# Key tiles 5, 6 and 7 of the product with V in one interleaved group, exponential 0 before the evacuation, small loads in step 0, and experts' products in pairs

## The reference

```python
x = L0_attn_resid_stream                       # (4, 1024, 128), f32
x = x + attn(layernorm(layernorm(x), ln_w, ln_b))
x = x + moe(layernorm(x))
# attn: 16 heads of 64, causal softmax(q k^T / 8) v, then W_o and b_o
# moe, token by token:
spikes_enc = sigmoid(y @ enc_W + enc_b)        # 128 -> 256
cont = spikes_enc @ s2c_W + s2c_b              # -> 64
logits = tanh(cont @ rW1 + rb1) @ rW2 + rb2    # -> 8 experts
w = top-2 of softmax(logits), scaled to sum 1
h = relu(cont @ We1[e] + be1[e]); out = sum_e w_e (h @ We2[e] + be2[e])
spikes_moe = sigmoid(out @ c2s_W + c2s_b)      # 64 -> 256
decoded = sigmoid(spikes_moe @ dec_W + dec_b)  # -> 128
result = layernorm(decoded, ln_g, ln_b)
```

## Time and profile before

| | us |
|---|---|
| median of 3 runs | 1065.34 |
| lowest and highest | 1065.0, 1068.29 |
| the profiled execution | 1063.64 |
| span of its trace | 1061.6 |
| busy PE, DVE, ACT, POOL | 1005.0, 863.3, 725.0, 739.3 |

### The profile page before, as it was taken

How to read it: one execution, slowest core, us unless ns; L and a number is a source line. 1 busy time by engine, 2 the same in 40 slices (tenths; PEclk the granted TensorE clock), 3 DMA queues, 4 the chain that set the end, 5 groups by cost and what they waited for, 6 DMA issues and landing times.

```text
span 1061.6 us, 50267 instructions
## 1 busy us (share of the span) xinstructions
PE 1005.0 (95%) x19084; PEld 760.5 (72%) x19084; DVE 863.3 (81%) x2052; ACT 725.0 (68%) x1540; POOL 739.3 (70%) x725
## 2 busy tenths in 40 slices
PE   4799999999999999999999999999999978999985
PEld 2577777777777777777777777777777766555543
DVE  6888888888888888888888888888888876557573
ACT  3666777777777777777777777777777755768673
POOL 5797777777777777777777777777777733444653
PEclk8999999999999999999999999999999988999997
DMA  7678888988888888888888888888888864132422
GB/s 164 165 202 212 208 211 205 207 207 208 206 205 204 208 205 205 206 203 203 204 204 204 205 202 205 203 205 201 204 201 206 207 137 87 42 91 51 99 51 69
DMA packets 133022, 188.78 MB, mean 178 GB/s; under 512 B 46976, under 2 KB 60288, under 8 KB 132992
## 3 DMA queue, kind: packets, MB, share of 16 engines
q1 hardware_dynamic: 132992, 188.40, 74.6%
HBM read 133.39 MB, written 21.36 MB: 146 GB/s over the span
## 4 chain that ended last, share of the span: by engine, by line
PE 62%; DVE 14%; issue 12%; DMA 4%; ACT 4%; POOL 2%; SPq 1%; ACTq 1%; DVEq 0%; POOLq 0%
PE ZB L758 24%; PE SPS L732 12%; PE SPS L733 9%; DVE PTZ L1056 5%; PE ZB L777 4%; DVE SSB L1094 3%; PE ZB L714 3%; PE ZB L784 3%; DMA VR<-gate_scratch 2%; ACT PRL L1394 2%; PE ZB L708 1%; DMA gate_scratch<-PRS 1%; POOL X L628 1%; PE SPS L916 1%; DVE PTZ L1251 1%
## 5 line engine op out<-in xcount | busy, mean ns | idle before, releaser
L1094 DVE CUSTOM_DVE_ANT_0 SSB<-SPS,MASK 128x640 f32<-128x640 f32 (+7 forms) x512 | 370.8, 746 | 60.0 <-issue 31.2
L1394 ACT ACTIVATE PRL<-SSB,NM 128x640 f32<-128x640 f32 (+3 forms) x256 | 253.3, 989 | 140.1 <-DVE NM L1094 140.1
L732 PE MATMUL SPS<-KHP,QS 128*128 (+3 forms) x768 | 306.8, 407 | 13.0 <-DVE NM L1094 7.8
L758 PE MATMUL ZB<-PTZ,VR 32*64 32x256 f32 (+3 forms) x12288 | 276.7, 306 | 6.5 <-DVE PTZ L1056 6.2
L1056 DVE STREAM_TRANSPOSE PTZ<-PRL 128x640 f32<-128x640 f32 (+3 forms) x256 | 257.6, 1025 | 0.1
L758 PEld LDWEIGHTS ZB<-PTZ,VR 32*64 32x64 f32 x12288 | 222.2, 131 | 49.2 <-issue 37.2
L733 PE MATMUL SPS<-KLP,QS 128*128 (+3 forms) x768 | 256.6, 343 | 0.0
L1394 ACT ACTIVATE PRS<-SSB,NM 128x128 f32<-128x128 f32 (+3 forms) x256 | 143.2, 562 | 90.3 <-DVE NM L1094 90.3
L732 PEld LDWEIGHTS SPS<-KHP,QS 128*128 128x128 f32 x768 | 145.5, 190 | 80.6 <-issue 47.5
L534 POOL TENSOR_TENSOR PTZ<-PTZ,RSB 128x512 f32<-128x512 f32 x64 | 81.2, 1292 | 132.5 <-ACT PTZ L1405 132.2
L515 POOL TENSOR_TENSOR QS<-RAW,QS 64x512 fp32r<-64x512 f32 x128 | 165.5, 1293 | 10.3
(11 more groups left out here) (178 smaller groups left out, 1215.8 us busy)
## 6 DMA issues: line engine op xcount, KB each, us to landing
VR<-v_scratch SPq DMA_DIRECT2D x248, 256.0 KB, 7.3
KHP<-KHP SPq DMA_DIRECT2D x64, 256.0 KB, 3.6
KLP<-KLP SPq DMA_DIRECT2D x64, 256.0 KB, 4.5
v_scratch<-V SPq DMA_DIRECT2D x32, 512.0 KB, 7.7
RSB<-rcp_scratch SPq DMA_DIRECT2D x64, 256.0 KB
XTB<-xt_scratch SPq DMA_DIRECT2D x62, 256.0 KB, 4.6
XW<-xt_scratch SPq DMA_DIRECT2D x30, 512.0 KB, 8.3
VR<-gate_scratch SPq DMA_DIRECT2D x32, 256.0 KB, 4.7
```

What stands on the lines that cost most here:

```text
L732: pe.matmul(SP_[n % 2][:, o + c0:o + c1], q, kh[:, c0:c1], start=True, stop=False)
L758: last = pe.matmul(ZB[h * DH:(h + 1) * DH, i, t0 * TR:QT * TR], VR[rows, j, kt, h * DH:(h + 1) * DH], turned_block(h, kt, j, rows, t0), st ...
L1094: v.tensor_tensor_reduce(out=SSB[n % 2][:, 0:w], in0=SP_[n % 2][:, o:o + w], in1=MASK[:, S - w:S], scale=1.0, scalar=BIG, op0=ALU.add, op1 ...
L1394: act.activation(exps_of(n), SSB[n % 2][:, 0:w], ACT.Exp, bias=NM[:, col:col + 1], scale=-1.0, accum_out=L[:, col:col + 1]).then_inc(exp_d ...
```

## The change

Five edits:
1. Values of key tiles 5, 6 and 7 are one group of `last_values`, in twelve rounds; its semaphore counts three tiles at its end. After step 31: values(4), logits, values(5,6,7).
2. In the steps of the loop ScalarE makes exponential 0 before it evacuates qk(0).
3. In the beginning the first spreads are split by head, scores(0) and (1) wait each for their own, and the statistics of batch 2 come ahead of the key splits.
4. Eleven small loads go to a new buffer SMALL (40 columns, set to zero once by VectorE) and are issued by SP in step 0, before `store_xt(2)`. `load_router` issues 9 loads instead of 15, `load_experts` 7 instead of 12.
5. In the chunks the hidden products come in pairs ahead of the experts' groups, and ScalarE's order follows.

```diff
-        ENCB, S2CB, RB1 = BV[:, 0:2], BV[:, 2:3], BV[:, 3:4]
-        RW2, RB2, BE1 = BV[:, 8:16], BV[:, 16:24], BV[:, 24:32]
-        C2SB, BE2 = BV[:, 32:34], BV[:, 64:64 + E // 2]
+        SMALL = sb("SMALL", [P, 40])
+        ENCB, S2CB, RB1 = SMALL[:, 0:2], SMALL[:, 2:3], SMALL[:, 3:4]
+        RW2, RB2, BE1 = SMALL[:, 8:16], SMALL[:, 16:24], SMALL[:, 24:32]
+        C2SB, BE2 = SMALL[:, 32:34], SMALL[:, 34:34 + E // 2]
...
             def store_xt(b):
                 sp.wait_ge(xt_ready, 2 * b + 2)
                 sp.dma_start(xt_dram[:, b * S:(b + 1) * S], XST[b]).then_inc(xt_stored[b], DMA)
-            spread(sp, 0, 0, 0)
+            for h in range(2):
+
+                sp.wait_ge(k_split, h + 1)
+                for x in (KH[0], KL[0]):
+                    sp.dma_start(x[0:DH, h, 0:CH].bitcast(F32), x[DH:P, h, 0:CH].bitcast(F32)).then_inc((head_spread, keys_spread[0])[h], DMA)
             sp.wait_ge(pool_const, 3)
             stage(sp, 1)
             spread(sp, 0, 0, 1)
...
                 spread_v(sp, it, half, par, 1)
                 store_v(sp, it + 1, 1 - par)
                 if first:
+                    load_small()
                     store_xt(2)
                     store_xt(3)
                     for b in range(1, B):
...
-                loads = [(ENCW, a["enc_W"]), (ENCB, a["enc_b"].rearrange("(m p) -> p m", p=P)),
...
-                         (C2SB, a["c2s_b"].rearrange("(m p) -> p m", p=P)),
-                         (S2CB[0:M], col(a["s2c_b"])), (S2CB[M:P], col(a["s2c_b"])),
...
-                         (RB1[0:M], col(a["rb1"])), (RB1[M:P], col(a["rb1"]))]
...
                     sp.dma_start(dst, src, allow_slow_non_contiguous=True).then_inc(f_loaded, DMA)
...
+            def load_small():
+                sp.wait_ge(small_set, 1)
+                loads = [(ENCB, a["enc_b"].rearrange("(m p) -> p m", p=P)),
+                         (C2SB, a["c2s_b"].rearrange("(m p) -> p m", p=P)),
+                         (S2CB[0:M], col(a["s2c_b"])), (S2CB[M:P], col(a["s2c_b"])),
+                         (RB1[0:M], col(a["rb1"])), (RB1[M:P], col(a["rb1"])),
+                         (RW2[0:M], a["rW2"]), (RB2, a["rb2"].partition_broadcast(P)),
+                         (BE1, a["be1"].rearrange("e h -> h e")),
+                         (BE2[0:M], a["be2"].rearrange("(p h) m -> h m p", h=2)[0]),
+                         (BE2[M:P], a["be2"].rearrange("(p h) m -> h m p", h=2)[1])]
...
+                    sp.dma_start(dst, src, allow_slow_non_contiguous=True).then_inc(f_small, DMA)
...
             def load_experts():
...
-                        [(RW2[0:M], a["rW2"]), (RB2, a["rb2"].partition_broadcast(P)),
-                         (BE1, a["be1"].rearrange("e h -> h e")),
-                         (W2, a["We2"].rearrange("e h m -> h e m")),
+                        [(W2, a["We2"].rearrange("e h m -> h e m")),
...
-                         (BE2[0:M], a["be2"].rearrange("(p h) m -> h m p", h=2)[0]),
-                         (BE2[M:P], a["be2"].rearrange("(p h) m -> h m p", h=2)[1]),
...
                     sp.dma_start(dst, src, allow_slow_non_contiguous=True).then_inc(f_late, DMA)
...
                 if last:
+                    gp.wait_ge(f_small, FFN_SMALL * DMA)
                     gp.wait_ge(f_loaded, FFN_LOADS * DMA)
...
-            if blocks == (QT - 2, QT - 1):
+            if blocks == (QT - 3, QT - 2, QT - 1):
...
-            work = [[(QT - 2, j) for j in range(n)] + [(QT - 1, j) for j in range(i + 1)] for i in range(n)]
-            for r in range(2 * n):
+            work = [[(QT - 3, j) for j in range(n)] + [(QT - 2, j) for j in range(n)] + [(QT - 1, j) for j in range(i + 1)] for i in range(n)]
+            for r in range(3 * n):
                 for i in range(n):
-                    done = [-(-len(work[i]) * k // (2 * n)) for k in (r, r + 1)]
+                    done = [-(-len(work[i]) * k // (3 * n)) for k in (r, r + 1)]
...
-            last.then_inc(pv_done, 2)
+            last.then_inc(pv_done, 3)
...
-                    if n in (0, UNITS // 2):
+                    if first and it == 0 and n < 2:
+                        pe.wait_ge((head_spread, keys_spread[0])[n], SPREADS * DMA)
+                        pe.wait_ge(q_split, n + 1)
+                    elif n in (0, UNITS // 2):
...
             values(3, 4)
...
-            values(5)
-            values(6, 7)
+            values(5, 6, 7)
...
             pe_values(pe, it, 2, 3)
...
-            pe_values(pe, it, 4, 5)
+            pe_values(pe, it, 4)
...
             pe_logits(pe, 0)
-            pe_values(pe, it, 6, 7)
+            pe_values(pe, it, 5, 6, 7)
...
                 pe_hidden(pe, c, par, 1)
                 if not last:
                     pe_encode(pe, c + 1)
-                pe_hidden(pe, c, par, 2)
                 if first:
+                    pe_hidden(pe, c, par, 2)
                     pe_out(pe, STEPS - 1, 0, Z)
                     pe_out(pe, STEPS - 1, 1, MB)
                     pe.wait_ge(out_copied, STEPS * 2 - 1)
-                pe_experts(pe, c, 0)
-                pe_hidden(pe, c, par, 3)
-                if not first:
+                    pe_experts(pe, c, 0)
+                    pe_hidden(pe, c, par, 3)
+                else:
+                    pe_hidden(pe, c, par, 2)
+                    pe_hidden(pe, c, par, 3)
+                    pe_experts(pe, c, 0)
                     pe_c2s(pe, c - 1, 0)
+                if not last:
+                    pe_cont(pe, c + 1)
                 pe_hidden(pe, c, par, 4)
-                if not last:
-                    pe_cont(pe, c + 1)
+                pe_hidden(pe, c, par, 5)
                 if not first:
                     pe_c2s(pe, c - 1, 1)
                 pe_experts(pe, c, 1)
-                pe_hidden(pe, c, par, 5)
                 if not last:
                     pe_router(pe, c + 1, 1 - par)
                 pe_hidden(pe, c, par, 6)
+                pe_hidden(pe, c, par, 7)
                 if not first:
                     pe_decode(pe, c - 1)
                 if not last:
                     pe_logits(pe, c + 1)
                 pe_experts(pe, c, 2)
-                pe_hidden(pe, c, par, 7)
                 if not last:
                     pe_norm_turn(pe, c + 2)
                 pe_experts(pe, c, 3)
...
+            v.memset(SMALL[:, :], 0.0).then_inc(small_set, 1)
             norm_stats(v, 0)
...
             norm_stats(v, 1)
+            norm_stats(v, 2)
             for s in range(2):
...
-            norm_stats(v, 2)
             norm_stats(v, 3)
...
                 exps_to(2, 7)
             else:
                 act_exp(act, it - 1, 1 - par, UNITS - 1)
+                exps_to(0, 1)
                 qk(0)
-                exps_to(0, 1)
                 qk(1)
                 exps_to(1, 2)
                 qk(2)
...
                 hidden(c, 3)
                 if not first:
                     out_hidden(c - 1, 0)
+                if not last:
+                    cont(c + 1, 1 - par)
                 hidden(c, 4)
-                if not last:
-                    cont(c + 1, 1 - par)
+                hidden(c, 5)
                 if not first:
                     out_hidden(c - 1, 1)
-                hidden(c, 5)
                 if not last:
                     routed(c + 1)
                 hidden(c, 6)
+                hidden(c, 7)
                 if not first:
                     decoded(c - 1)
                 if not last:
                     exps(c + 1)
-                hidden(c, 7)
                 if not last:
                     turn_of(c + 2)
                 if first:
```

More of the change, by code:

```diff
@@ L218, in build_program @@
         keys_spread = [sem(f"keys_spread{c}") for c in range(2)]
+        head_spread = sem("head_spread")
         qk_filled = sem("qk_filled"); qk_evac = sem("qk_evac")
@@ L231, in build_program @@
         out_filled = sem("out_filled"); out_copied = sem("out_copied"); out_evac = sem("out_evac")
+        small_set = sem("small_set"); f_small = sem("f_small")
         f_loaded = sem("f_loaded"); f_late = sem("f_late"); f_high = sem("f_high"); f_weights = sem("f_weights"); zeroed = sem("zeroed")
@@ L284, in staged_count @@
             return it * (3 * DMA) + 2 * DMA
-        FFN_LOADS, FFN_LATE = 15, 12
+        FFN_SMALL, FFN_LOADS, FFN_LATE = 11, 9, 7
         def stage_x(sp, it, c):
@@ L434, in load_router @@
                 sp.wait_ge(zeroed, 2)
-                loads = [(ENCW, a["enc_W"]), (ENCB, a["enc_b"].rearrange("(m p) -> p m", p=P)),
+                loads = [(ENCW, a["enc_W"]),
                          (S2CW[:, :, 0:M], a["s2c_W"].rearrange("(m p) c -> p m c", p=P)),
@@ L438, in load_router @@
                          (DECW, a["dec_W"].rearrange("(m p) d -> p m d", p=P)),
-                         (C2SB, a["c2s_b"].rearrange("(m p) -> p m", p=P)),
-                         (S2CB[0:M], col(a["s2c_b"])), (S2CB[M:P], col(a["s2c_b"])),
```

(20 more changed lines are left out.)

## The result

The changed kernel takes 1056.69 us (median of 4 runs, 1054.79 to 1058.98) against 1066.82 for the kernel before beside it: a ratio of 0.9911, 95% interval 0.9884 to 0.9939. That is 9.5 us less, with an interval from 6.5 to 12.4. The forecast was 1056.4. Run once more beside three variants, it gave 1058.16 and 0.9924 (0.9895 to 0.9954).

A forecast was written before the change was run, and what follows sets the result against it. PE, busy 756.9 of the attention loop's 763 us, was taken to bind. Terms -7.8 - 1.5 + 1.9 - 1.5 + 0 + 0 = -8.9 took 1063.64 to 1054.7; 1.7 for the median gave 1056.4 us, range 1048.0 to 1063.0.

The forecast's parts named there:

- the cover by mask(1): VectorE in the loop: with exponential 0 early, mask(2) is held only by mask(1), starting at 508.47, not 509.01.
- the 0.27: PE before values(0) in the loop: 0.27 us per step free to win, 29 x 0.27 = -7.8 us.
- GpSimd's addition as the cover of the late evacuation: Loop: qk(0)'s evacuation comes about 0.6 us later, but GpSimd, its reader, is adding outputs from 508.35 to 510.86.
- no difference: Rival for the whole kernel: the loop's 0.27 does not arrive and the load chain costs; 1064.2 us, chance 0.09.
- no wait behind the later semaphore: Loop: tile 5's semaphore comes some 1.1 us later for VectorE's transpose of unit 10; cost 0, 0.3 us cover.
- a token 0.05 per step: Loop, values of key tiles 5, 6, 7 in one group: 0.05 us saved per step, -1.5 us in all.
- columns that bind: Rival on the group of tiles 5, 6, 7: half or more of 0.60 us won, 1048.6 or below; chance 0.12.
- 15.4 ns a record: Rival on the group of tiles 5, 6, 7: slower than 12.4 ns, +15.5 us, total 1073.4; chance 0.07.
- the small loads in step 0: Eleven loads on SP ahead of X's stores delay values(0) of step 2: +1.9 us, ends 0 and +6.8.
- stores late: Step 0: X's first store moves from 53.34 to 60.1, so the stores land at 65.3 instead of 63.3.
- fewer and earlier transfers should shorten it: Last step, PE's 3.39 us stall in the last values group: shortened by -1.5 us, ends 0 and -3.4.
- PE's 6.1 us of waits lie beside it: Experts' chunks: the gates' loop sets the period, not PE's relu waits; term 0, ends -6.1 and +1.0.

The follow-up runs named there:

- the last experiment: Kernel before with exponential 0 early and experts' pairs, plus the experts' twelve loads issued behind V's four pieces: 1056.87 us, ratio 0.9905.
- the single runs: Kernel before with one edit alone each: exponential 0 early 1057.75 us, values of tiles 5, 6, 7 1067.01, small loads 1068.32, experts' pairs 1062.04.

## Why the prediction was right or wrong

**Right: exponential 0.** Forecast -7.8 in the loop, measured -7.5 there and, by the runs, -7.1 for the whole kernel (-4.5 to -9.8 by the interval). The working held step by step: the cover by mask(1), the 0.27 of which 0.07 is overlap, GpSimd's addition as the cover of the late evacuation. The rival "no difference" falls with it.

**Right: no wait behind the later semaphore.** PE waits for nothing in the loop of the changed kernel, so if the transpose of unit 10 and mask(13) come later, it does not reach PE.

**Wrong in sign, small: the interleaved group.** Forecast -1.5, measured +0.03 per step, some +1 in all. The step that failed is "a token 0.05 per step": a gain was booked for which no row spoke. Both rivals on this group, columns that bind and 15.4 ns a record, fall: it takes 12.6 ns a record (2.12 / 168). The choice of the nearest row was right, the discount on it was not. By the rule of the Trainium skill ("TensorE: Matmul & The Clock Gate", Part 3, The mechanism), that matmuls start and end in program order, the prediction had worked out 0 here, nearer than mine, though the mixed starts of the earlier trace rows still speak against its wording.

**Mis-sized: the small loads in step 0.** Forecast +1.9. By the means above +2.7 at values(0) of step 2, and +4.7 in the run of that edit alone against the profile of the kernel before (92.2 against 87.5). Two numbers were too low: the eleven issues took 8.35 us rather than 6.8, and SP went on 6.8 us after the issue of the first store (69.47 - 62.67) rather than 5.1. The run with the loads behind the stores shows that the step "stores late" holds only a part: SP then still goes on 1.9 us later than without the loads (means of 66.4 and 64.4), held by its own issues; with the loads ahead of the stores it is 3.9.

**Wrong: the last step.** Forecast -1.5 for a shorter stall. The stage to chunk 0 is 45.8, 45.8, 46.5, 47.4, 43.6 and 46.8 with fewer loads there, 47.9, 46.2, 46.4, 44.4, 47.8, 46.2 and 45.7 with all of them in their place: means 46.0 and 46.4. The stall itself is 1.6 to 3.4 us in the one group (mean 2.4) and 2.4 to 4.2 in the other (3.2): 0.7 by the means, with the two overlapping. The step that failed is "fewer and earlier transfers should shorten it": the stall was read as traffic of these loads, and the last experiment refutes that for the experts' part of them. The prediction's other word for it, that PE waits for its next instructions, is what the packets bear out. The 2.2 us between the two profiles is within this spread.

**Wrong: the experts' pairs.** Forecast 0, measured -2.3 in chunks 1 to 7 (means of 107.4 and 105.1) and -2.9 in the runs. The step that failed is "PE's 6.1 us of waits lie beside it": it was right for the one execution that was read, in which PE never held VectorE back after chunk 1. In three other kernels with the same order of the chunks it did, in eight of 15 stretches; a PE that is 94% busy in that stage was too near to the bound to be called beside it. The window over the chunks of the kernel before (columns as in the earlier trace rows) said so, 133.46 of 142.30 us:

```profile
902.30:1044.60 142.30, 133.46 (x566) 72.17 (x566) 87.67 (x268) 102.33 (x159) 72.97 (x61) 0.99 0.30 71
```

The low end of that term, -6.1, held it.

**The beginning.** Forecast 0; nothing can be told from the runs. The trace shows the first mask 0.9 us later, inside the ends of that term.

**Its own signs.** Two signs that it had named for being wrong came: values(0) of step 2 is more than 4 us late (5.5), and the chunks have another period. Of its signs for being right SP's wait ended at 69.5 rather than near 65, the step is 26.2 rather than 26.1, and the group takes 2.12, a little above its 2.0 to 2.1.

In sum -7.8 - 1.5 + 1.9 - 1.5 + 0 = -8.9 was forecast. By the single runs it is -7.1 + 1.4 + 3.2 - 2.9 = -5.4; by the profiles -6.0; by the runs of the changed kernel -9.5 and -8.1, each with some 3 us to either side. That the median came within 0.3 us of the forecast is luck: the pairs cancel against the loads, the group and the last step, and scatter of some 3 us does the rest.

## What to carry to other kernels

Ask of the one wait on the binding engine what short operation stands in front of its releaser on another engine: exchanging two operations on ScalarE, which is busy 68% of the time, was worth more than all the rest. Before a loop over a transfer is called the bound, look at the same wait in every round and in more than one execution; two loops of nearly equal length show it by rounds that differ. And an edit that brings a start forward (scores(0) here, by 2 us) pays only if the next reader was waiting for it.

## What the runs showed that was not expected

The steps of kernels with the same order in the loop differ by up to 0.04 us for the length of a run: 26.167 (exponential alone, and with the experts' loads late), 26.200, 26.202 and 26.206 in the others without the interleaved group, 26.200 to 26.247 with it. Over 28 steps that is 1.1 us, as much as the interleaved group costs; its cause is open. The time from the last step's values(0) to chunk 0 varies by 4.4 us between kernels (43.6 to 47.9) that differ little there, and eleven small loads delay what follows even when they are issued behind the transfers that are waited for. And a stall of TensorE that the view of waits names only "issue" could be dated to an instruction packet among the DMA packets.
